# Two FFNs whose first chunk is prepared one stage earlier, and K and Q projections of two batches at once in fp32r parts

## The reference, cut to what matters

```
x = layernorm(x + gather_conv(x))        # L0 attention: 8 heads, 32 taps, linear interpolation
x = layernorm(x + moe_gelu(x))           # L0 FFN: own layer norm, 8 experts 128->512->128, top 2, "abel" branch
x = layernorm(x + attention(x))          # L1 attention: 16 heads of 8, softmax(q k^T / sqrt(8)) v, projection
x = layernorm(x + moe_silu(x))           # L1 FFN: 8 experts 128->256->128 with silu(h) * g, top 2
```

## Time and profile before

| | |
|---|---|
| median of 3 runs | 869.27 us |
| the runs | 881.5, 865.5, 869.27 us |
| the profiled execution | 877.47 us |
| its span | 875.7 us |
| mean granted TensorE clock | 0.865 of full |
| busy: PE, DVE, ACT, POOL | 697.6, 670.6, 501.6, 114.5 us |

### The profile page before, as it was taken

One profiled execution on the slowest core, in us unless ns is written; L12 is line 12 of the kernel. 1 busy time (PEld: TensorE's weight loads), 2 busy tenths in 40 slices (PEclk: granted clock), 3 DMA queues, 4 the chain that ended last, 5 costly groups with the idle time before them and its releaser, 6 DMA issues. The chain is left out here.

```text
span 875.7 us, 14793 instructions
## 1 busy us (share of the span) xinstructions
PE 697.6 (80%) x5418; PEld 549.5 (63%) x5418; DVE 670.6 (77%) x1464; ACT 501.6 (57%) x926; POOL 114.5 (13%) x91
## 2 busy tenths in 40 slices
PE   6375766666377899999999767788887869999996
PEld 4255655555375667778778544455454448888886
DVE  3998899999935797989979856887777137777765
ACT  4767576877525476866768425675665524234232
POOL 1113122213303560000000063000000000000000
PEclk9987787867675998999989867998888669999998
DMA  7453333444403411003020040000000000000000
GB/s 229 115 139 105 93 111 102 117 112 133 120 26 111 137 49 63 35 1 98 1 65 33 0 145 1 1 1 1 2 1 1 1 1 1 1 13 1 13 13 12
DMA packets 76699, 48.30 MB, mean 55 GB/s; under 512 B 54994, under 2 KB 64980, under 8 KB 76628
## 3 DMA queue, kind: packets, MB, share of 16 engines
q1 hardware_dynamic: 73268, 44.75, 17.5%
q10 hardware_dynamic: 3360, 2.62, 1.0%
HBM read 37.85 MB, written 9.50 MB: 54 GB/s over the span
## 5 line engine op out<-in xcount | busy, mean ns | idle before, releaser
L918 ACT ACTIVATE hT<-hps,b1s 128x512 f32<-128x512 f32 x128 | 87.9, 692 | 63.4 <-PE hps L829 60.7
L1084 DVE TENSOR_TENSOR hl<-hT,hh 128x512 fp32r<-128x512 f32 x128 | 91.7, 738 | 29.6 <-ACT hh L924 28.0
L1492 DVE TENSOR_REDUCE mx<-s_ps 128x2 f32<-128x512 f32 x128 | 82.6, 688 | 39.2 <-PE s_ps L1263 38.5
L1428 ACT ACTIVATE pt<-st_ps 128x512 f32<-128x512 f32 x128 | 69.8, 603 | 42.2 <-PE st_ps L1273 42.0
L1693 ACT ACTIVATE act_h<-up 128x512 f32<-128x512 f32 x64 | 38.3, 598 | 89.7 <-PE up L1646 89.7
L313 ACT ACTIVATE rest<-rest,par 128x264 f32<-128x264 f32 x128 | 53.7, 502 | 36.8 <-DVE rest L561 36.8
L306 ACT ACTIVATE tap<-cst_s,par 128x328 f32<-128x328 f32 x128 | 72.3, 653 | 3.8 <-DVE par L614 3.8
L1777 DVE TENSOR_TENSOR hid<-act_h,up 128x512 f32<-128x512 f32 x64 | 43.3, 685 | 27.9 <-PE up L1646 17.1
L1657 PEld LDWEIGHTS eo<-wc,hid 128*128 128x128 f32 x512 | 61.7, 192 | 2.3
L1657 PE MATMUL eo<-wc,hid 128*128 128x128 f32 x512 | 62.1, 275 | 0.0
L924 ACT CAST hh<-hT 128x512 fp32r<-128x512 f32 x96 | 59.2, 617 | 0.0
(11 more groups left out here) (255 smaller groups left out, 1704.6 us busy)
## 6 DMA issues: line engine op xcount, KB each, us to landing
kd<-kst SPq DMA_DIRECT2D x16, 512.0 KB, 2.6
xc<-in_x_coarse SPq DMA_DIRECT2D x16, 512.0 KB, 4.0
wdB<-wdd SPq DMA_DIRECT2D x32, 256.0 KB, 5.2
dW<-kd SPq DMA_DIRECT2D x16, 256.0 KB, 3.3
Ks<-kd SPq DMA_DIRECT2D x64, 33.0 KB, 2.1
dW<-kd SPq DMA_DIRECT2D x64, 32.0 KB, 2.1
w1r<-in_w ACTq DMA_DIRECT2D x5, 256.0 KB, 2.7
w2r<-in_w ACTq DMA_DIRECT2D x5, 256.0 KB, 3.2
```

Source lines behind the costliest of these rows:

```text
L918: nc.scalar.activation(hT[k][:], hps[:, k, :], ACT.Gelu, bias=b1s[:, m:m + 1]).then_inc(h_done, 1)
L1084: nc.vector.tensor_tensor(hl[s % 2][:, k, :], hT[k][:], hh[s % 2][:, k, :].bitcast(F32), ALU.subtract).then_inc(hl_done, 1)
L1428: nc.scalar.activation(pt[h % 8][:].rearrange("p t q -> p (t q)"), st_ps[k][:], ACT.Exp, scale=SCALE)\
L1492: nc.vector.tensor_reduce(mx[:, :, h:h + 1], s_ps[k][:].rearrange("p (t k) -> p t k", t=2), AX, ALU.max).then_inc(s_used, 1)
```

## The change

Five things are changed.

1. **FFN 0's chunk 0 is prepared in stage 1.** The tiles `xnT0`, `xnh0`, `xnl0`, `xh0`, `twice0` and `lg` are now made in `build`. PE turns the rows at the end of n = 14, makes the turn back behind `out_rows(14)` and the logits behind `gathered(15)`; ACT does the root, the rows and the high part between its copies of tiles 14 and 15; DVE does its part behind its last tile. The block of FFN 0 begins with `up(0)` on PE and `chosen(0)` on DVE. ACT's first table load there is that of gelu.
2. **FFN 1's chunk 0 is prepared in attention** in the same way: statistics in round 8, root, rows, turn, columns and high part in round 9, the low part at the end. The tiles are shared with those of FFN 0.
3. **K and Q are projected in fp32r parts for two batches at once.** `project(n)` makes three fp32r matmuls of 512 columns (high x high, high x low, low x high) for one group of four heads of two batches. The counts stay: 32 projections in all. `high` and `split` are one operation of 512 columns each instead of two of 256. `qf` and `kf` are two buffers of 512 columns instead of three of 256. The first six projections stand at the front, then four in each of the rounds 0 to 5 and two in round 6.
4. **POOL splits what this needs**: `wqk` behind the last expert's weights, and the columns of chunks 0 and 1 of the result during FFN 0 (`columns_split`); those of chunks 2 and 3 in attention.
5. **Attention's front in order of need**: the first projections come ahead of the bias row, which now stands behind the first scores.

```diff
@@ PE, stage 1
                     if n >= 1:
                         gathered(n - 1)
+                    if n == NT - 2:
+                        pe.wait_ge(o_used, R8)
+                        for t in range(TC):
+                            last = nc.tensor.transpose(turn[:, t * P:(t + 1) * P], sT[:, t * P:(t + 1) * P], ident[:])
+                        last.then_inc(rows0, 1)
...
                 out_rows(NT - 2)
+                pe.wait_ge(xh0_done, 1)
+                for t in range(TC):
+                    last = nc.tensor.transpose(kps[1][:, t * P:(t + 1) * P], xh[0][:, t, :], ident[:])
+                last.then_inc(xhT0_ready, 1)
                 gathered(NT - 1)
+                pe.wait_ge(xn0_ready, 1)
+                for t in range(TC):
+                    last = nc.tensor.matmul(turn[:, t * E:(t + 1) * E], xnT[0][:, t * P:(t + 1) * P], gw[:],
+                                            start=True, stop=True)
+                last.then_inc(lg0_ready, 1)
                 out_rows(NT - 1)
@@ FFN 0: POOL
             for q in range(1, Q):
                 ...
+                if q >= 2:
+                    columns_split(q - 2)
@@ FFN 0: PE
-            rows_of(0)
-            normalised(0)
-            logits(0)
@@ FFN 0: ACT
-            nc.scalar.activation(warm[:], eps_t[:], ACT.Sqrt)
-            roots(0, ONE, TWO + 1)
-            rows_normalised(0)
-            rows_high(0)
+            nc.scalar.activation(warm[:], eps_t[:], ACT.Gelu)
@@ attention: PE
+            def project(n):
+                p, g, which = part_of(n)
+                if p >= 2:
+                    pe.wait_ge(yT_ready, 2 * (p - 1))
+                xh_, xl_ = (xTh, xTl) if p < 2 else (yTh, yTl)
+                for k, (w, x) in enumerate(((wqkh[:, which, g, :], xh_), (wqkh[:, which, g, :], xl_), (wqkl[:, which, g, :], xh_))):
+                    last = nc.tensor.matmul(bank_of(n)[:], w, x[:, (p % 2) * 2 * L:(p % 2 + 1) * 2 * L],
+                                            start=(k == 0), stop=(k == 2))
...
+                if i == B + 1:
+                    pe.wait_ge(x3_0, 1)
+                    for t in range(TC):
+                        last = nc.tensor.transpose(s_ps[0][:, t * P:(t + 1) * P], total[0][:, t, :], ident[:])
+                    last.then_inc(x3T_0, 1)
@@ attention: DVE
+            for i in range(ROUNDS):
                 largest(i, 0)
+                if i == 0:
+                    split(2)
+                    split(3)
                 projected(i - 3)
+                if i == B + 1:
+                    first_rows()
+                if i == B:
+                    first_rows_stats()
                 largest(i, 1)
+                if i == 0:
+                    split(4)
+                    split(5)
+                split(4 * i + 6)
                 largest(i, 2)
```

More of the change, by code:

```diff
@@ L1230, in _ @@
         def _(pe):
-            def project(b, which, pair, x):
-                for j in range(2):
-                    last = nc.tensor.matmul(x_ps[x][:, j * L:(j + 1) * L], wqk[:, which, 2 * pair + j, :],
-                                            xT_all[:, b * L:(b + 1) * L], start=True, stop=True)
+            def project(n):
[6 more added lines that the diff above has]
+                                            start=(k == 0), stop=(k == 2))
                 last.then_inc(proj_ready, 1)
@@ L1402, in _, with high @@
         def _(act):
-            def high(n, which, pair):
+            def high(n):
+                if n >= PROJ:
+                    return
+                p, g, which = part_of(n)
                 act.wait_ge(proj_ready, n + 1)
@@ L1455, in _ @@
                 powers(i - 1, 4)
[L1456 to L1457 removed]
+                high(4 * i + 8)
                 powers(i - 1, 5)
```

358 lines of the change are left out of this document (217 added, 141 removed).

## The result

| | before | after |
|---|---|---|
| median, us | 877.7 (20 runs, 865.5 to 888.9) | 862.96 (20 runs, 855.5 to 866.2) |
| ratio | | 0.9858, 95% interval 0.9825 to 0.9892 |
| profiled execution, us | 877.47, span 875.7, clock 0.865 | 864.53, span 862.7, clock 0.854 |

The change makes the kernel 1.4% faster by the ratio and 1.7% by the medians, so it stays within 2% of no change. The ratio leaves out the runs that lie over 1.5% above the fastest of their kernel, 8 of the 20 before; the medians are of all runs. The prediction said 851.4. With 20 runs the kernel before stands at 877.7, where its profiled execution was, and not at the 869.3 of the three runs shown.

A forecast was written before the change was run, and what follows sets the result against it. It took PE to bound both FFNs apart from their starts, and a DVE-PE loop over score banks plus the clock to bound attention. Terms -6.8 + 1.3 + 0.6 - 6.6 - 6.4 = -17.9 us gave 859.6, or 851.4 median; range 840 to 866.

The forecast's parts named there:

- FFN 0's start: Seam of stage 1 and FFN 0: preparation chain replaced by a barrier, 6.8 us won (4.5 to 8).
- (a): Stage 1's end: four new transposes ahead of `turned(14)` cost 0.8 us, the relay behind them having no slack.
- (c): Stage 1's end: logits ahead of the last `out_rows` cost 1.3 us, between full cost at low clock and half.
- POOL's new work: FFN 0: POOL's added splits, 7.6 us of work, slow DVE's `hl`; 1.3 us lost (0 to 2.6).
- Attention's front and round 0: From last `sT` to round 1's first maxima: first scores 1.9 us sooner, round 0 longer; 0.6 us lost in sum.
- I get 2.5 us more: Attention's round 0: four more DVE splits and PE's wait for the bias row's copy lengthen it by 2.5 us.
- Rounds 1 to 7: Attention: shorter projections, high parts and splits save 0.84 us a round; 6.6 us won at unchanged clock (3 to 9).
- FFN 1's start: Seam of attention and FFN 1: `up` follows the last sum within 0.35 us; 6.4 us won.
- A: Rival, attention's rounds: clock falls oftener, mean about 0.78, seven rounds lose 10 to 12 us; 871.1 or 862.9; chance 0.18.
- B: Rival, FFN 0: PE waits for expert weights at `up(1)` or later, all 6.8 us come back; 866.4 or 858.2; chance 0.15.
- C: Rival, attention's rounds: clock stays low once fallen, mean 0.70, kernel slower than before; 884.5 or 876.3; chance 0.05.
- D: Rival: PE's idle gaps at the fronts go, clock falls shrink by 8 us; 851.6 or 843.4; chance 0.12.

The follow-up runs named there:

- experiment 2: Changed kernel with ACT's copy of the bias row ahead of its high parts 4 and 5 instead of behind them; 857.40 us, ratio to before 0.9747.
- the one with halves: Changed kernel with ACT's high part and DVE's split of each projection again as two instructions of 256 columns; 869.11 us, ratio to before 0.9913.
- the mended kernel with float32 projections: The three mended with each projection again one float32 matmul of 512 columns; 858.11 us, ratio to before 0.9832.
- the seams alone: Changed kernel with before's attention put back, both FFNs' moved beginnings kept, POOL's four FFN 1 weight instructions held; 863.72 us, once more 864.41 us.
- experiment 4: Changed kernel with K/Q weight split one chunk later, bias row copied earlier, POOL's FFN 1 weight instructions held behind negated maxima; 852.62 us, once more 850.72 us.
- the three mended: Changed kernel with K/Q weight split later, bias row copied earlier and POOL's FFN 1 weight work held; 852.62 and 850.72 us, twelve-run median 851.3.

## Where the prediction was right, and where it failed

**The base.** The step "I take the excess for clock luck" failed: 877.5 was the usual time of the kernel before, 869.3 a draw of three. Against 877.5 the sum said 859.6. The miss of 11.6 us is 8.2 of base and 4.9 of terms, less 1.5 by which the median after lies under its own profiled execution. A median of three runs that spread by 16 us is no level to set against a profiled execution. The change itself, forecast at 17.9 us, was 14.7 by the medians and 12.4 by the ratio.

**FFN 0's start, right and too small.** The mechanism held: up(0) 0.7 us behind the last `sT` starts, `up(1)` with the slack as computed. Terms (a) and (c), 2.1 us together, came out at 0.3, and that is in part luck: in this execution the clock rose sooner (0.72 instead of 0.56 from 243 to 247 us). In the five profiles where it rose as late as before, term (a)'s 0.8 us is there at the end of the 16 transposes (0.7 to 0.9), and 0.2 to 0.9 us are left at the last `sT`.

**POOL's new work, mis-sized: 4.0 instead of 1.3.** The step that failed is "0.22 us for each us of POOL", a slope from the mean of `hl` (1087 and 688 ns). The mean came from a mixture of untouched and held instructions, and what counts is how long the POOL instruction is that one of them meets. The work itself was 9.0 us where 7.6 were estimated. Over all profiled executions with FFN 0's beginning moved, the last sum comes at 492.4 with the split in place (six, 490.4 to 494.9), at 489.6 with it one chunk later (five, 488.5 to 491.6), at 487.7 with no split and no columns (three, 487.0 to 488.0). So all of POOL's new work costs 4.7 us, beyond the upper bound of 2.6 and below the 7.6 of a full block for every us; 2.7 of it is the place of one cast and one subtraction. The Trainium skill (SBUF — State Buffer, Who interferes with whom) says that one engine holds the shared port pair for the whole instruction while the other fully blocks, and that a `tensor_scalar` out of SBUF into SBUF can take the pair as well. The trace agrees to 0.1 us, with 521.56 + 1.72 beside 521.36 + 1.89 above and 4.26 us on 16 columns. The prediction's sentence dropped a condition of the Trainium skill: an instruction with one SBUF input is untouched only outside the modes that use both ports. Rule and rows were both in hand; the prediction took the mean of the rows.

**Attention's front and round 0, mis-sized: 5.6 instead of 0.6.** The front won 1.3 of the 1.9 us forecast; round 0 lost 6.9 where "I get 2.5 us more" stood. Four things. The bias row's copy, named there among the reasons for "by hand I get 2.5 us more", alone costs 1.8 (experiment 2). The hold of the negated pair, 3.5 us instead of 0.6, was not in the list: the prediction said that attention's maxima and splits read PSUM and lose nothing, which is right, and left out the two instructions of 16 columns that don't. Mending it gave 2.0 to 2.3 us (23.16 to 20.85 and 21.14). The splits between the first maxima cost about the 3.0 us that the prediction had for them: with the row mended the first two steps still take 3.3 and 3.5 us instead of 1.9 and 2.0, and the second takes 3.52 in all new kernels but the one with halves, whether round 0 has a mean clock of 0.59 or 0.84. That alone is more than the 2.5 us by hand, which so had nothing for the row's wait and the pair. The last three steps are longer where the clock is lower: 2.2, 2.3 and 2.6 us at the 0.61 of the changed kernel's round 0, 1.9, 1.9 and 2.2 at the 0.84 of the mended kernel with float32 projections. With before's own attention code the seams alone make round 0 20.84 us at 0.51, instead of 18.13 at 0.81. Why the low level lasts longer there is open.

**Rounds 1 to 7: the full-clock round right, the sum close in part by luck (5.8 against 6.6).** "A full-clock round near 18.8" came out as 18.78, 0.84 shorter. In the sum, rounds 1 to 6 won 7.6 us where 5.2 were forecast, and round 7 lost 1.8 where 1.4 were to be won; the same code in two profiles (experiment 4) differs by 5.6 us there. The split of the 0.84 was wrong too. Steps 1, 2, 3 and 0 became 0.16, 0.26, 0.24 and 0.18 us shorter, where 0.37, 0.2, 0.17 and at most 0.1 had been counted: three fp32r matmuls hold the queue 0.89 us from first to the next scores (574.17 to 575.06), not 0.69, and ACT's one instruction takes 0.78 us, not the 0.59 of a plain copy.

**FFN 1's start, right: 6.5 against 6.4.** Another 1.4 us went in FFN 1 itself, where nothing was forecast; its mean clock was 0.99 instead of 0.97.

**The rivals.** A has 862.9 us, the time that came out, but that is coincidence: its mean clock of 0.78 didn't come (0.86). B's wait at `up(1)` is 0.39 us; its thought, that FFN 0's gain is exchanged for another wait, came half true, but through DVE. C and D did not come. The range of 840 to 866 held the time, but only because it was wide: the forecast's own bounds, 843 to 861, didn't. "Within 2%" (0.57) was the case.

**Where the expected gain went.** As it was written, the new attention part gives nothing: the kernels without it have medians of 862.0 and 864.4 us, the changed kernel has 863.0. Once three places are mended, in none of which the arithmetic changes, the kernel stands at 851.3. How much of that is the new attention is open. By the medians it is about 13 us (864.4 against 851.3); by the ratios, 0.9737 and 0.9812 without it and 0.9732 and 0.9729 with it, it is between nothing and 7 us. Some 6 us are work at the full clock, 0.84 us a round. That the rest comes from the clock in the rounds is argued, not shown.

## What to carry to other kernels

Before you move work to an idle GpSimd, list VectorE's instructions with all operands in SBUF in that stretch: each can stand for the rest of the GpSimd instruction that it meets, however small it is itself. Hold that GpSimd work behind a semaphore of the last such instruction, and put it where VectorE has slack; cutting it to pieces moved FFN 0's last sum to 487.3 from 489.0 here, without a better median. Read single rows, not the mean of a group; and set a sum made on one profiled execution against many runs, not three.

## What the hardware showed that was not expected

- A VectorE instruction of 128x16 took 4.26 and 4.42 us instead of 0.17 and 0.19, beside GpSimd subtractions of 4.5 us, and was booked as busy without any wait. VectorE instructions with one operand in PSUM stayed at 686, 741 and 680 ns beside the same subtractions.
- TensorE's granted clock differs between executions and kernels that run the same code: rounds 1 to 6 of before's attention took 118.9 us at a mean of 0.95 and 128.2 at 0.87, those of the three mended 116.8 at 0.92 and 122.4 at 0.85. A round is 19.62 us with no fall (2.4 GHz throughout), and 21.14 or 23.23 at means of 0.92 and 0.78, with a part at 1.2 GHz. So a gain of a few us in one pair of profiles can be the clock's.
- Sixteen transposes at the end of stage 1 took 1.9 to 3.3 us in 15 profiles of the same code, by when in them the clock rose from 0.50 to 1.00 (244.02 to 246.94).
